# List counts one step later as bf16 products, lists zeroed batch by batch, expert rows read ahead of the stage's barrier

## The reference

```python
scores_BSN = jnp.einsum('bsd,nd->bsn', x, Wr) + br
_, idx_BSK = jax.lax.top_k(scores_BSN + biases_N[None, None, :], K)        # K = 2, N = 8 experts
h_NM2H = jnp.einsum('md,ndh->nmh', x_MD, Wl1) + bl1[:, None, :]
y_NMD = jnp.einsum('nmh,nhd->nmd', jax.nn.silu(a_NMH) * b_NMH, Wl2) + bl2[:, None, :]
y_MD = jnp.einsum('mn,nmd->md', ew_MN, y_NMD)                              # weights of the chosen experts
```

## Time and profile before

| | us |
|---|---|
| median of 3 runs | 998.56 |
| lowest, highest run | 996.36, 1004.04 |
| the profiled execution's own time | 994.61 |
| its span in the trace | 992.7 |

### The profile page before, as it was taken

How to read it: one execution, slowest core, us unless ns; L and a number is a source line. 1 busy time by engine, 2 the same in 40 slices (tenths; PEclk the granted TensorE clock), 3 DMA queues, 4 the chain that set the end, 5 groups by cost and what they waited for, 6 DMA issues and landing times. The chain is left out here.

```text
span 992.7 us, 26217 instructions
## 1 busy us (share of the span) xinstructions
PE 891.3 (90%) x8784; PEld 758.1 (76%) x8785; DVE 612.0 (62%) x1561; ACT 469.1 (47%) x1209; POOL 379.8 (38%) x555
## 2 busy tenths in 40 slices
PE   4888889777999999997999899999999999779995
PEld 3677667636999999995556598888888887667784
DVE  3588788754455555542017466768667686549895
ACT  3777777712222222221333444445444454349895
POOL 4477677530000000006101446445464444426762
PEclk9998999987999999998999999999999999879998
DMA  4454447432433333315765798897989986411121
GB/s 119 145 164 145 143 148 237 140 145 94 128 108 93 98 93 108 93 44 181 262 225 180 165 188 185 179 182 164 200 172 176 172 178 150 90 33 55 60 61 49
DMA packets 222059, 137.78 MB, mean 139 GB/s; under 512 B 160289, under 2 KB 207393, under 8 KB 221857
## 3 DMA queue, kind: packets, MB, share of 16 engines
q1 hardware_dynamic: 180304, 99.78, 40.1%
q10 hardware_dynamic: 38608, 28.64, 10.8%
q0 software_dynamic: 3072, 8.39, 2.6%
HBM read 81.79 MB, written 54.98 MB: 138 GB/s over the span
## 5 line engine op out<-in xcount | busy, mean ns | idle before, releaser
L1717 ACT ACTIVATE c_pT<-c_T 128x512 f32<-128x512 f32 (+2 forms) x90 | 50.2, 595 | 104.4 <-PE c_T L1876 73.3
L1666 POOL TENSOR_TENSOR c_soft<-c_soft,c_share 128x616 f32<-128x616 f32 (+2 forms) x96 | 70.3, 760 | 63.4 <-DVE c_share L2129 61.8
L1062 ACT ACTIVATE b_rowsT<-b_RT 128x256 f32<-128x256 f32 x39 | 15.0, 383 | 158.2 <-PE b_RT L1104 158.2
L1173 DVE COPY b_w<-moe_w 128x1024 f32 x78 | 53.5, 687 | 56.2 <-issue 50.7
L1676 POOL MEMSET d_round<- 128x1 f32 x1 | 0.1, 98 | 226.5 <-POOLq L953 226.5
L1113 PEld LDWEIGHTS b_G<-b_rowsT,b_w 128*128 128x128 f32 x624 | 77.2, 195 | 4.2 <-DVE b_w L1173 1.5
L1113 PE MATMUL b_G<-b_rowsT,b_w 128*128 128x128 f32 x624 | 77.9, 279 | 1.5 <-ACT b_rowsT L1062 1.3
L1113 PE MATMUL b_U<-b_rowsT,b_w 128*128 128x128 f32 x624 | 76.1, 275 | 0.0
L1187 DVE SCALAR_TENSOR_TENSOR b_hidT<-b_U,b_bias,b_gate 128x128 f32<-128x128 f32 x156 | 43.9, 343 | 51.9 <-PE b_U L1113 45.4
L1140 PE MATMUL b_Y<-moe_w,b_hidT 128*128 x312 | 73.9, 380 | 0.9 <-DVE b_out L1218 0.9
L1113 PEld LDWEIGHTS b_U<-b_rowsT,b_w 128*128 128x128 f32 x624 | 72.9, 192 | 0.0
(11 more groups left out here) (231 smaller groups left out, 2167.2 us busy)
## 6 DMA issues: line engine op xcount, KB each, us to landing
rel_windows<-c_relw ACTq DMA_DIRECT2D x28, 368.0 KB, 6.7
c_bias<-rel_windows SPq DMA_DIRECT2D x16, 616.0 KB, 5.6
prob_rows<-c_soft SPq DMA_DIRECT2D x16, 616.0 KB, 7.3
moe_w<-in_L_Wl SPq DMA_DIRECT2D x16, 512.0 KB, 4.1
early<-in_L_early SPq DMA_DIRECT2D x16, 384.0 KB, 3.2
values<-c_pT ACTq DMA_DIRECT2D x22, 256.0 KB, 3.8
b_rows<-expert_lists SPq DMA_DIRECT2D x39, 128.0 KB, 2.0
expert_out<-b_out SPq DMA_DIRECT2D x39, 128.0 KB, 1.7
```

Of the source, the lines that this page charges most:

```text
L1173: nc.vector.tensor_copy(own[p][h][:, :, :], w1[:, bass.ds(e, 1), :, h * HE:(h + 1) * HE].rearrange("p o c n -> p (o c) n"))\
L1666: ins = nc.gpsimd.tensor_tensor(soft[p][:, hs, a:z], soft[p][:, hs, a:z], share[:, s, hs].unsqueeze(2).to_broadcast([P, HS, z - a]), ALU.mult)
L1717: nc.scalar.activation(dst, view(T[k]), ACT.Copy, **kw).then_inc(g["emptied"], 1)
```

## The change

1. `places` and the five list instructions move from the end of step b to the following step, so that step b now holds them for batch b-4. On PE `places(b-4)` stands behind the transposes of the attention output and the first of the probabilities, ahead of the scores; on DVE the list instructions stand behind L766, ahead of the maxima L754; on POOL the scatter stands at the head of the step. There is one more step, 19.
2. `chosen`, the triangle and the ones of `places` are bfloat16; POOL copies the triangle once at the start.
3. The lists are zeroed ahead: in step b SP writes zeros into rows b*128 to b*128+127 of all eight lists (`fill`, one DMA of 1 MB), 16 times; scatter waits for the fill of its batch. `pad`, `padded` and L920 are gone.
4. SP issues the loads of the first two tiles inside `layer0`, as soon as the rows of the tiles are known and all scatters have landed; DVE reads the first two expert numbers there too. ACT copies and stores all four of the last early results.

```diff
+            def fill(b, i, p):
+                since(sp, s_fill[p], 16 * i)
+                block_rows = t["lists"].rearrange("(e r) d -> r e d", e=NE)[bass.ds(b * P, P)]
+                sp.dma_start(block_rows, zeros[:, :].unsqueeze(1).to_broadcast([P, NE, D])).then_inc(s_fill[p], 16)
 
             def steps(b, i, p):                                   # SP
                 if there(b + 2):
                     load_context(b + 2, p)
+                if there(b):
+                    fill(b, i, p)
                 if there(b + 4):
                     load(b + 4, p)
...
             by_batch(steps)(sp)
-            pad(sp, 0)
-            for n in range(EARLY_HALVES - 4, EARLY_HALVES - 2):
-                text_store(sp, n, text_dv, n - 3)
-            padded(sp, 0)
-            for out in shared["s_text_out"][:2]:
-                sp.wait_ge(out, 16 * EARLY_HALVES // TEXT_BANKS)
+            sp.wait_ge(s_tiles, 1)
+            for p in range(2):
+                sp.wait_ge(s_sc[p], 32 * (NB // 2))
+            for n in range(2):
+                shared["load_rows"](sp, n, n)
...
             def steps(b, i, p):                                   # POOL
+                if there(b - 4):
+                    if there(b - 2):
+                        apart(pool, g["p_sb"], 4 * (b - 2) + HPT)
+                    scatter(b - 4, i - 2, p)
                 if there(b + 3):
                     std(0, b + 3)
...
-                if there(b - 3):
-                    if there(b - 1):
-                        apart(pool, g["p_sb"], 4 * (b - 1) + HPT)
-                    scatter(b - 3, 1 - p)
...
-                nc.tensor.matmul(T[1][:, D + NE:D + 2 * NE], before, chosen[:, :], start=True, stop=True)
-                nc.tensor.matmul(T[1][:, D + 2 * NE:D + 3 * NE], ones, chosen[:, :], start=True, stop=True)\
+                nc.tensor.matmul(T[1][:, D + NE:D + 2 * NE], before_b[:, :], chosen[:, :], start=True, stop=True)
+                nc.tensor.matmul(T[1][:, D + 2 * NE:D + 3 * NE], ones_b[:, :], chosen[:, :], start=True, stop=True)\
...
                 if behind:                                        # DVE
                     attention_out(den)
+                if listed:
+                    row = list_rows(b - 4, list_counts(b - 4))
+                    list_slots(b - 4, i - 2, p, list_sums(b - 4, row))
                 if there(b):
                     maxima(b, 0)
...
                 if behind:
                     rows_normal(b - 2, i - 1, p)
-                if lists:
-                    row = list_rows(b - 3, list_counts(b - 3))
-                    list_slots(b - 3, i - 2 + p, 1 - p, list_sums(b - 3, row))
```

More of the change, by code:

```diff
@@ L163, in cst @@
             return const[:, a:z]
-        ident, before, ones = cst("ident"), cst("before"), cst("ones")
+        ident, before = cst("ident"), cst("before")
         wq = sb("a_wq", [P, KD, D])
@@ L287, in run @@
                         steps(i * 2 + p, i, p)
-                for b in range(NB - 4, NB + 3):
+                for b in range(NB - 4, NB + 4):
                     steps(b, b // 2, b % 2)
@@ L302, in text_halves @@
         def text_halves(b):
-            return {NB: range(0, 1), NB + 1: range(1, 3), NB + 2: range(3, 4)}[b]
+            return {NB: range(0, 1), NB + 1: range(1, 3), NB + 2: range(3, 4), NB + 3: range(0)}[b]
         block = ctx.enter_context(nc.Block())
[L307 to L315, removed]
         def text_part(n):
@@ L409, in residual, with scatter @@
                 nc.gpsimd.tensor_tensor(x_res[p][:, :], x_res[p][:, :], beta[:, :], ALU.add).then_inc(g["res"], 1)
-            def scatter(b, p):
+            def scatter(b, i, p):
+                apart(pool, s_fill[p], 16 * (i + 1))
                 apart(pool, g["slot"], b + 1)
@@ L679, in steps @@
                     probabilities(b - 1, 1 - p, 0)
+                if there(b - 4):
+                    places(b - 4)
                 if there(b):
@@ L868, in steps @@
             def steps(b, i, p):
-                front, ahead, behind, lists = there(b + 3), there(b + 1), there(b - 2), there(b - 3)
+                front, ahead, behind, lists, listed = there(b + 3), there(b + 1), there(b - 2), there(b - 3), there(b - 4)
                 if behind:
@@ L941, in _ @@
             fin(nc.vector.scalar_tensor_tensor(tr[:, :], tt[:, :], float(P), tr[:, :], ALU.mult, ALU.add))
-            nc.vector.tensor_copy(shared["tile_row"][:, :], tr[:, :])
+            nc.vector.tensor_copy(shared["tile_row"][:, :], tr[:, :]).then_inc(s_tiles, 1)
             fin.end()
[L944 to L948, removed]
+            shared["first_experts"] = [shared["expert_of"](dve, n) for n in range(2)]
 def experts(nc, t, shared):
@@ L967, in experts @@
         tile_expert, tile_row = shared["tile_expert"], shared["tile_row"]
-        rows = [sb(f"b_rows{p}", [P, D]) for p in range(2)]
+        rows = shared["rows"]
         rowsT = [sb(f"b_rowsT{p}", [P, KD, P]) for p in range(2)]
@@ L989, in experts @@
         s_clear = sem("b_clear")
-        s_in = [sem(f"b_in{p}") for p in range(2)]
+        s_in = shared["s_rows"]
         s_out = [sem(f"b_out_{p}") for p in range(2)]
@@ L1018, in _ @@
         def _(sp):
[L1019 to L1022, removed]
-                sp.dma_start(rows[p][:, :], t["lists"][bass.ds(row, P)]).then_inc(s_in[p], 16)
             def store(n, p):
@@ L1029, in steps @@
             def steps(n, i, p):
-                load(n, p)
+                if not isinstance(n, int) or n > 1:
+                    shared["load_rows"](sp, n, p, g["rt_mm"])
                 if there(n - 3):
@@ L2598, in load_experts, with expert_of, load_rows @@
                               one(t["L0_Wl2"])[:, half * HE // 2:(half + 1) * HE // 2].rearrange("e (k p) n -> p (e k) n", p=P)).then_inc(s, 16)
+            shared["rows"] = [moe.enter_context(nc.sbuf_tensor(f"moe_rows{p}", [P, D], F32)) for p in range(2)]
+            shared["s_rows"] = [ctx.enter_context(nc.semaphore(f"s_rows{p}")) for p in range(2)]
+            def expert_of(eng, n):
+                at = shared["tile_expert"][0:1, n:n + 1] if isinstance(n, int) else shared["tile_expert"][0:1, bass.ds(n, 1)]
+                return eng.value_load(at, min_val=0, max_val=NE - 1)
+            shared["expert_of"] = expert_of
+            def load_rows(sp, n, p, read=None):
+                at = shared["tile_row"][0:1, n:n + 1] if isinstance(n, int) else shared["tile_row"][0:1, bass.ds(n, 1)]
+                row = sp.value_load(at, min_val=0, max_val=NE * ROWS_E - P)
+                if read is not None:
+                    since(sp, read, n - 1)
+                sp.dma_start(shared["rows"][p][:, :], t["lists"][bass.ds(row, P)]).then_inc(shared["s_rows"][p], 16)
+            shared["load_rows"] = load_rows
             shared["experts_ready"] = 16 * 4 * NE
```

39 lines of the change are left out of this document (16 added, 23 removed).

## The result

The changed kernel takes 1004.25 us (median of 20 runs), the kernel before 996.73 (20 runs): a ratio of 1.0076, interval 1.0058 to 1.0095. It is 7.5 us slower. The forecast was 1009.0, in a range of 995 to 1020, with 10.4 us of loss. The kernel before has medians from 994.8 to 999.0 us in the five sets of runs of this study, so a kernel is compared only with the runs of the kernel before that were taken beside it.

The account below looks back on a forecast made before the run. A ring of input landing, DVE, POOL and next load was taken to bound the steps. 11.8 (lists, scatter) + 1.6 (landings) - 3.0 (passage) = +10.4 us; on the median of 998.56 that gave 1009.0, range 995 to 1020.

Parts of the forecast that it names:

- The ring: Steps 4 to 12: input landing, DVE, POOL's `std(1)` and masks, next load form a closed chain, 11.23 us a step.
- The lists in the ring: DVE, steps 4 to 12: list instructions between L724 and L754 add 1.1 us a step, bounds 0.86 and 1.36.
- the 1.0 that step 6 gets back: DVE, step 6: the lists fill the 1.03 us that L754 waited for PE's scores, taken off the loss.
- The late scatter: POOL, steps 4 to 12: scatter behind the lists makes `std(1)` 0.5 us late a step, bounds 0 and 1.0.
- The landings: Input loads, steps 4 to 12: zeroing DMAs delay them slightly, 0.2 x 8 = 1.6 us.
- The last steps and the passage: Steps 16, 17 to expert products: row numbers some 1.2 us late, hidden; rows landed by the barrier, gain 3.0 us.
- Products at nothing: PE, `layer0` steps: bf16 products placed earlier remove 15.4 us of waits, yet are worth 0 alone.
- PE is the bound: Rival, `layer0` steps: each removed PE wait shortens its step, -15.4 - 3.0, or 980.2 us; chance 0.10.
- the forecast's own mechanism: Steps 4 to 12: lists and scatter lengthen the chain from landing to next load; chance 0.52, range 1004 to 1016.

Follow-up runs that it names:

- work ahead and behind: Two kernels: the changed kernel with three idle DVE statistics in steps 4 to 12, ahead of L718 (ratio 1.007) or behind it, before the list instructions (1.017).
- lists first: Changed kernel with DVE's five list instructions moved to the head of its step, ahead of L718: ratio 0.992.
- lists back: Changed kernel with places, list instructions and scatter at the end of their step again, as in the kernel before: ratio 0.993.
- half of the scatter: Changed kernel with one of the scatter's two DMAs, so only first-expert rows are written: ratio 1.0016.
- move alone: Kernel before with only places, list instructions and scatter moved to the next step, without fills: ratio 1.0131.
- float32 kernel: Changed kernel with the products of `places` back in float32: ratio 1.0088.
- ring open: Input statistics put behind the first two maxima; changed kernel with places, lists and scatter at their step's end: 0.9937; with only the lists at DVE's step head: 0.9873.

## Why the prediction came out as it did

**The ring: right.** The changed kernel starts L718 when the landing allows, in all nine steps. The work ahead and behind, the lists first, and the lists back all gave what the ring says. In the kernel before the ring holds in most steps, but not in all. In steps 7 and 12 L724 follows L762 by 0.17 us without idle, and in step 12 the mask had landed 3.0 us after its issue at 147.89, some 0.7 us before L724 started. DVE had idled there earlier, with no releaser in the profile (the earlier trace rows has L724's row):

```profile
151.42 0.26 DVE L762 RECIPROCAL early<-a_T 128x16 f32<-128x16 f32 x1 [0.40 <-issue]
151.59 0.37 DVE L724 BATCH_NORM_STATS2 early<-early 128x6 f32<-128x256 f32 x1
```

The five pieces of the ring can be added up over all eight turns, from the timelines of both kernels:

| piece, eight turns, us | before | changed | difference | forecast |
|---|---|---|---|---|
| input statistics to first maxima (the lists) | 6.45 | 13.80 | +7.35 | +7.8 |
| those to `std(1)` (the scatter) | 28.96 | 35.03 | +6.07 | +4.0 |
| `std(1)` to the mask's issue | 30.37 | 30.65 | +0.28 | 0 |
| mask's issue to the next statistics (the landing) | 27.52 | 24.24 | -3.28 | +1.6 |
| sum | 93.30 | 103.72 | +10.42 | +13.4 |

**The lists in the ring: right.** With the 1.0 that step 6 gets back they were forecast at 7.8 and came out at 7.35. A single step other than step 6 adds 0.68, 1.01 or 1.27, where 1.1 was taken for each. The reason I gave for staying below the upper bound, 1.36, was only half right. POOL was idle and L839 took 0.18 us, as in the earlier trace rows, but in the hardware loop the five stand apart, with register instructions recorded between them. In step 4, which is written out, they take 0.68 (61.39 to 62.07), in the longer steps of the loop 1.28 (138.88 to 140.16).

**The late scatter: right in kind, too small.** The step shown above has 0.66, where 0.5 was taken; over the eight turns it is 6.07 against 4.0, or 0.76 a step. In steps 4 and 5 the piece grew by 1.13 and 0.80. In the step shown `std(0)` and `std(1)` start 1.06 apart (143.42 and 144.48), where the prediction took 0.93. The kernel with half of the scatter shows that this term is real.

**The landings: mis-sized, with the wrong sign.** I added 1.6 us for later landings. In steps 4 to 12 of the changed kernel mask issue and statistics lie 2.96 to 3.10 us apart. In the kernel before, the nine distances are 3.0 to 4.5, 3.40 in the mean. The sum was made on the kernel's mean step of 11.66, which held 3.3 us above the usual 3.03 a turn, with parts taken from its shortest step; I counted those as if they had to come back. About 0.8 of the 3.3 is DVE's own lateness in steps 7 and 12, and the rest, mainly 0.8 in step 5 and 1.5 in step 9, is waiting for the load. So the forecast of 13.4 for these steps missed the 10.4 by -4.9 here, +2.1 at the scatter, -0.4 at the lists and +0.3 elsewhere: the largest error was partly made good by another. Why the kernel before has late landings and the changed one has none is open. They came with the move alone as well (5.21 once), so they are not tied to the old order. Both of those kernels have no fills and take 27.4 or 27.5 us in this piece, and the seven kernels with one fill a step that still wait at this place take 24.2 to 25.8; no run separates the fills from the rest of what sets the two groups apart.

**The last steps and the passage: nearly right.** From step 12 to the first products I had -3.0, and they took 78.19 and 75.68, so -2.5. From the last row numbers to the products 4.3 us are gained, and the forecast's own times give 4.2 there (3.0, and the 1.2 of lateness hidden in it). The last steps lose 1.8, where 1.2 had been forecast.

**The start: missed.** The prediction has no term for it. Step 4 begins 2.4 us later in the profile. With one fill a step the kernels stand at 58.7 to 61.4, without at 58.3 to 60.1, with two at 63.0. A part of it is the fills; how much, these single profiles do not settle.

**Products at nothing: right for this change.** The float32 kernel shows it for the number format, and lists back against lists first (0.993 and 0.992) for the place of the products. With the ring open the move has a price, 3.4 us in the eight steps, and PE's wait is the likely reason. "PE is the bound" lost as a rival.

**The number.** The time lay in the range, the sign was that of the forecast, and the loss came out at 0.76%, within the 1% that I gave 0.40, where slower by over 1% had 0.50. It is just inside the 1004 to 1016 that the forecast's own mechanism was given. 1.8 of the distance to 1009.0 is the base: the three runs shown had a median of 998.56 and twenty have 996.73. The other 2.9 has no single term. In the profiles the steps came out 3.0 under the forecast, the last steps and the passage 0.5 over it, the start 2.4 and the rest of the kernel 2.8, and the profiles overstate the timed loss by 5.6. That 10.4 stands both for the whole forecast and for the steps as measured is a coincidence.

## What to carry to other kernels

A load that reuses a buffer closes a ring through every engine that must release it. Find the instruction that waits for the landing, and see whether it starts exactly one landing after the issue: if so, work placed ahead of it is free, as long as it is shorter than the wait, and work placed behind it costs its length, less the slack of the engine that it stands on (the five list instructions on DVE cost all of theirs, the scatter on POOL 0.76 of its 2.4 us). A large wait on the busiest engine can be worth nothing while another ring paces the step; open that ring first, and it may be worth something (here 3.4 us, where the wait added up to 15.4).

## What was not expected of the hardware

- A DMA of 1 MB from the on-chip memory to DRAM in rows of 1 KB each step, 8.6 us to its landing in the median, left the masks behind it, issued at most 0.2 us before it landed, at 3.0 us. Twice as much made three of eight 3.7 to 4.0 us.
- The same chain of five small DVE instructions took 0.68 us in written-out code and 1.01 or 1.28 in turn in a hardware loop, where register instructions are recorded between them.
- Three independent DVE statistics with records of 0.42 us put off the next instruction by 0.99 us and not by 1.27.
- With the input statistics later, the kernel whose PE waits at one point of each step had a granted clock of 0.94 over 90 us, and the one without that wait 1.00. With the landing in the ring the same move left it at 0.94.
